# Second pass: factors turned by TensorE and multiplied from PSUM; node stage: P ahead of Q

## What is computed

```
z    = concat(h[src], h[dst], edge_feats) @ W.T + b          # 256 columns per edge
z    = (z - mean) * rsqrt(var + eps) * gamma + beta          # over all edges
msg  = sigmoid(z[:, :128]) * softplus(z[:, 128:])
x    = x + (h + zeros.at[src].add(msg))                      # summed by src
```

## Time and profile before

| | |
|---|---|
| median of 3 runs | 3818.71 us (3814.67 to 3823.7) |
| profiled execution | 3811.82 us, its span 3810.0 us |
| mean granted TensorE clock | 0.836 of 2.4 GHz |
| busy share | PE 68%, DVE 49%, ACT 37%, POOL 67% |
| chain that ended last, by engine | POOL 37%, PE 31%, issue 15%, DVE 7%, DMA 5%, ACT 3% |

### The profile page before, as it was taken

How to read it: one execution, slowest core, us unless ns; L and a number is a source line. 1 busy time by engine, 2 the same in 40 slices (tenths; PEclk the granted TensorE clock), 3 DMA queues, 4 the chain that set the end, 5 groups by cost and what they waited for, 6 DMA issues and landing times.

```text
span 3810.0 us, 64994 instructions
## 1 busy us (share of the span) xinstructions
PE 2572.3 (68%) x14952; PEld 1728.3 (45%) x14953; DVE 1875.5 (49%) x4083; ACT 1418.7 (37%) x2638; POOL 2552.8 (67%) x2545
## 2 busy tenths in 40 slices
PE   1788888778888885788888899972212113656348
PEld 1466666645555553344444444431111113555348
DVE  7555655555656566533333333343323234666448
ACT  3333333220000002322222222228877777777700
POOL 4477777467777660477777777755777777777730
PEclk9998999969989897999999999995555556887669
DMA  4233333335545451688888888877665555777358
GB/s 115 67 101 102 101 102 100 122 94 173 180 159 178 161 187 39 205 292 290 285 289 293 285 287 287 290 234 286 217 214 186 196 205 208 269 272 254 113 171 266
DMA packets 339096, 749.99 MB, mean 197 GB/s; under 512 B 66424, under 2 KB 130268, under 8 KB 333856
## 3 DMA queue, kind: packets, MB, share of 16 engines
q1 hardware_dynamic: 242656, 497.83, 37.8%
q0 software_dynamic: 93440, 218.82, 19.3%
q10 hardware_dynamic: 2880, 32.11, 2.2%
HBM read 465.29 MB, written 283.22 MB: 196 GB/s over the span
## 4 chain that ended last, share of the span: by engine, by line
POOL 37%; PE 31%; issue 15%; DVE 7%; DMA 5%; DVEq 3%; ACT 3%; POOLq 0%; SPq 0%; ACTq 0%
POOL m_tab L811 19%; POOL H L780 9%; PE PS L1554 9%; POOL arena L780 8%; PE PS L1564 8%; PE PS L1740 3%; PE PS L1627 2%; PE PS L1550 2%; DMA m_tab<-Q,pos_i 2%; DMA Q<-base_tab 1%; DVEq L1136 1%; PE PS L1609 1%; PE PS L1693 1%; PE PS L1719 1%; DVEq L409 1%
## 5 line engine op out<-in xcount | busy, mean ns | idle before, releaser
L780 POOL DMA_INDIRECT Q<-h_tab,src_i x960 | 954.8, 995 | 405.8 <-issue 273.7
L811 POOL DMA_INDIRECT m_tab<-Q,pos_i x784 | 833.7, 1063 | 275.2 <-issue 234.1
L1749 PE MATMUL PS<-ident,arena 128*128 128x128 f32 x784 | 196.2, 399 | 690.9 <-DVE arena L1452 608.4
L780 POOL DMA_INDIRECT arena<-p_tab,src_i x400 | 381.2, 953 | 262.8 <-DMA p_tab<-arena 141.2
L984 ACT ACTIVATE arena<-PS,LB 128x512 f32<-128x512 f32 x392 | 247.9, 683 | 746.7 <-PE PS L1724 746.7
L1564 PE MATMUL PS<-Q 128*128 x2684 | 420.0, 302 | 147.7 <-DVE Q L1138 65.0
L1749 PEld LDWEIGHTS PS<-ident,arena 128*128 128x128 f32 x784 | 129.0, 200 | 751.1 <-issue 529.0
L1564 PEld LDWEIGHTS PS<-Q 128*128 128x128 f32 x2684 | 355.3, 205 | 234.2 <-issue 229.9
L780 POOL DMA_INDIRECT H<-p_tab,src_i x384 | 363.9, 948 | 117.0 <-issue 116.1
L1724 PE MATMUL PS<-arena,WC 128*128 128x512 f32 x784 | 369.4, 594 | 0.0
L1719 PE MATMUL PS<-H,Q 128*128 x1464 | 352.7, 383 | 0.0
(11 more groups left out here) (231 smaller groups left out, 4351.8 us busy)
## 6 DMA issues: line engine op xcount, KB each, us to landing
z_tab<-arena SPq DMA_DIRECT2D x196, 512.0 KB
Q<-z_tab SPq DMA_DIRECT2D x196, 512.0 KB, 6.0
Q<-m_tab SPq DMA_DIRECT2D x234, 264.0 KB, 3.8
arena<-in_edge_t SPq DMA_DIRECT2D x196, 256.0 KB, 3.3
m_tab<-arena SPq DMA_DIRECT2D x48, 792.0 KB
m_tab<-src_i SPq DMA_DIRECT2D x112, 264.0 KB
arena<-dst_tab SPq DMA_DIRECT2D x196, 128.0 KB, 4.1
count_tab<-Q SPq DMA_DIRECT2D x11, 1568.0 KB
```

The source lines that it names most:

```text
L780: nc.gpsimd.indirect_dma_start(row(s, k), None, table, bass.IndirectOffsetOnAxis(src_i[:, t:t + 1], 0)).then_inc(landed[s], 16)
L811: nc.gpsimd.indirect_dma_start(m_tab, bass.IndirectOffsetOnAxis(pos_i[:, t:t + 1], 0), mrow[:, s, k, :], None).then_inc(ms.scattered[s], 16)
L1749: ins = turn(PS[:, 2 + q, t * P:(t + 1) * P], msg_t[:, q, t * P:(t + 1) * P], ident[:])
```

## The change

Node stage. TensorE makes all of P first (14 pieces of 4 and 3 tiles, 256 columns each) and then all of Q (21 pieces, 256 columns each, the blocks in the order 4, 5, 6, 0, 1, 2, 3), in three sets of two PSUM banks. The turned h stays whole in the arena (`ht_all`). VectorE adds h to X right after the layer norm, ahead of its part of Q, and the second rest of Q is written as part 2 in one instruction where there were two. GpSimd waits for the stored P and for `x_merged`; the first four groups are gathered into H, the next four into the arena, where each waits until the turned h under it is used up. The edge loads of pass 1 wait for nine pieces of Q.

Pass 2. ScalarE makes max(z, 0) itself (`positive`, a Relu into `core`). TensorE turns three things a group instead of one (`turn_parts`): the gate into banks 2 and 3, and into banks 0 and 1 the positive part and, added to it in PSUM by a plain multiplication with the identity, the logarithm. VectorE (`message`) copies the turned gate to SBUF, multiplies it with the sum in PSUM straight into `mrow`, and writes the source numbers. `scale_z`, `soften` and `take_rows` are gone. The seven output blocks have a buffer each.

```diff
             def turned_h(i):
                 act.wait_ge(pq.turned, i + 1)
-                if i >= 2:
-                    act.wait_ge(pq.product, len(SUBS) * (i - 1))
-                nc.scalar.copy(ht[:, i % 2, :], banks(0)).then_inc(pq.evicted, 1)
+                nc.scalar.copy(ht_all[:, i * NB:(i + 1) * NB, :]..., banks(0)).then_inc(pq.evicted, 1)
...
             gather_all(h_tab[1], conv_row, conv[1].group_done, CITER * CS, rows_landed[0:CS], DG)
             all_stored(pool, pq.p_stored)
+            pool.wait_ge(p1.x_merged, NI)
             gather_all(p_tab, p_row, p1.done, SL, rows_landed, 0)
...
+            def positive(d, s):
+                nc.scalar.activation(core[s], zin[:, s, GE:2 * GE], ACT.Relu, bias=bn[:, 11:12], scale=bn[:, 9:10]
+                                     ).then_inc(ms.relu_ready, 1)
...
-                    v.tensor_tensor(q_rest(c - 1), q_rest(c - 1), q_part(c - 1, 1), ALU.subtract
-                                    ).then_inc(dn.rest[1], 1)
-                    dve.wait_ge(dn.rest[1], SPLIT + c)
-                    v.tensor_copy(q_part(c - 1, 2), q_rest(c - 1)).then_inc(dn.part[2], 1)
+                    v.tensor_tensor(q_part(c - 1, 2), q_rest(c - 1), q_part(c - 1, 1), ALU.subtract
+                                    ).then_inc(dn.part[2], 1)
...
             def message(d, s):
                 g, q = group_of(d, s), s % 2
-                dve.wait_ge(ms.soft_ready, g + 1)
-                dve.wait_ge(ms.turned, g + 1)
-                v.tensor_tensor(msg_t[:, q, :], gate[:, s, :], soft[:, s, :], ALU.mult).then_inc(ms.msg_t_ready, 1)
+                dve.wait_ge(ms.turned, g + (RZ + 1))
+                if not (isinstance(d, int) and d == 0):
+                    dve.wait_ge(ms.scattered[s], eight_of(d) * (16 * GT))
+                v.tensor_copy(gate_rows[:, q, :], PS[:, 2 + q, :]).then_inc(ms.gate_taken, 1)
+                dve.wait_ge(ms.gate_taken, g + 1)
+                v.tensor_tensor(mrow[:, s, :, 0:F], PS[:, q, :].rearrange("p (a b) -> p a b", b=F),
+                                gate_rows[:, q, :].rearrange("p (a b) -> p a b", b=F), ALU.mult)
+                v.tensor_copy(mrow[:, s, :, F:F + 1].rearrange("p a b -> p (a b)"), columns(src_f, g)
+                              ).then_inc(ms.row_ready, 1)
...
-            def turn_msg(d, s):
+            def turn_parts(d, s):
                 g, q = group_of(d, s), s % 2
-                pe.wait_ge(ms.msg_t_ready, g + (RZ + 1))
+                pe.wait_ge(ms.relu_ready, g + (RZ + 1))
                 pe.wait_ge(ms.row_ready, g + 1)
                 for t in range(GT):
-                    ins = turn(PS[:, 2 + q, t * P:(t + 1) * P], msg_t[:, q, t * P:(t + 1) * P], ident[:])
+                    turn(PS[:, 2 + q, t * P:(t + 1) * P], gate[:, s, t * P:(t + 1) * P], ident[:])
+                for t in range(GT):
+                    mm(PS[:, q, t * P:(t + 1) * P], core[s][:, t * P:(t + 1) * P], ident[:], is_transpose=True,
+                       start=t == 0, stop=False, skip_group_check=True)
+                pe.wait_ge(ms.ln_ready, g + 1)
+                for t in range(GT):
+                    ins = mm(PS[:, q, t * P:(t + 1) * P], soft[:, s, t * P:(t + 1) * P], ident[:],
+                             start=False, stop=True, skip_group_check=True)
                 ins.then_inc(ms.turned, 1)
```

More of the change, by code:

```diff
@@ L772, in gather_all @@
                     s = (g - first) % depth
-                    if table is p_tab and g == SL:
-                        pool.wait_ge(p1.x_merged, NI)
+                    if table is p_tab and SL <= g < RP:
+                        last = (g - SL + 1) * GT * H2 // F - 1
+                        pool.wait_ge(pq.product, CP + len(SUBS) * (Q_ORDER.index(last // NB) + 1))
                     if g >= first + depth:
@@ L961, in _ @@
             turned_h(0)
-            for c in range(CH):
-                i, (j0, j1) = c // len(SUBS), SUBS[c % len(SUBS)]
+            for c in range(CP):
+                i, (j0, j1) = c // len(QUADS), QUADS[c % len(QUADS)]
+                if j0 == 0 and i + 1 < NI:
+                    turned_h(i + 1)
                 act.wait_ge(pq.product, c + 1)
@@ L966, in _ @@
                     act.wait_ge(pq.p_stored[i % 2], 16 * (i // 2))
-                nc.scalar.copy(p_s[:, i % 2, j0 * H2:j1 * H2].rearrange("p (j f) -> p j f", f=H2), pq_bank(c, 0)
+                nc.scalar.copy(p_s[:, i % 2, j0 * H2:j1 * H2].rearrange("p (j f) -> p j f", f=H2), p_bank(c)
                                ).then_inc(pq.p_ready, 1)
-                nc.scalar.copy(q_part(c, 0), pq_bank(c, 1)).then_inc(dn.part[0], 1)
-                if j0 == 0 and i + 1 < NI:
-                    turned_h(i + 1)
+            for c in range(CH):
+                act.wait_ge(pq.product, CP + c + 1)
+                nc.scalar.copy(q_part(c, 0), q_bank(c)).then_inc(dn.part[0], 1)
                 if c >= 1:
@@ L1014, in logarithm @@
                 nc.scalar.activation(soft[:, s, :], soft[:, s, :], ACT.Ln, bias=1.0).then_inc(ms.ln_ready, 1)
-            def take_rows(d, s):
-                g, q = group_of(d, s), s % 2
-                act.wait_ge(ms.turned, g + 3)
-                if not (isinstance(d, int) and d == 0):
-                    act.wait_ge(ms.scattered[s], eight_of(d) * (16 * GT))
-                nc.scalar.copy(mrow[:, s, :, 0:F], PS[:, 2 + q, :].rearrange("p (a b) -> p a b", b=F))
-                nc.scalar.copy(mrow[:, s, :, F:F + 1].rearrange("p a b -> p (a b)"), columns(src_f, g)
-                               ).then_inc(ms.row_ready, 1)
             def four(d, s, stage):
@@ L1487, in _ @@
                 dve.wait_ge(fin.turned, i + 1)
-                if i >= 3:
-                    dve.wait_ge(fin.out[i % 3], 16 * (i // 3))
-                v.tensor_tensor(outs[:, i % 3, :], banks(4 + i % 2 * 2), node_tiles(X, i), ALU.add
+                v.tensor_tensor(outs[:, i, :], banks(4 + i % 2 * 2), node_tiles(X, i), ALU.add
                                 ).then_inc(fin.added, 1)
@@ L1688, in _ @@
                 pe.wait_ge(pq.evicted, i + 1)
-                if c >= 2:
-                    pe.wait_ge(dn.rest[0], SPLIT + c - 1)
+                if c >= QB:
+                    pe.wait_ge(pq.p_ready, c - QB + 1)
                 for j in range(j0, j1):
-                    bank = PS[:, 2 + 3 * (c % 2) + j - j0, :]
-                    ins = mm(bank, ht[:, i % 2, j * F:(j + 1) * F], WAB[:], start=True, stop=True)
+                    ins = mm(p_bank(c)[:, j - j0, :], ht_all[:, i * NB + j, :], WAB[:, 0:H2], start=True, stop=True)
+                ins.then_inc(pq.product, 1)
+            pe.wait_ge(pq.p_ready, CP)
+            for c in range(CH):
+                t, n = pq_tiles(c)
+                if c >= QB:
+                    pe.wait_ge(dn.rest[0], SPLIT + c - QB + 1)
+                for j in range(n):
+                    ins = mm(q_bank(c)[:, j, :], ht_all[:, t + j, :], WAB[:, H2:2 * H2], start=True, stop=True)
                 ins.then_inc(pq.product, 1)
```

108 lines of the change are left out of this document (44 added, 64 removed).

## The result

| | before | changed |
|---|---|---|
| median of 8 runs each | 3815.36 us (3809.45 to 3823.7) | 3802.86 us (3792.84 to 3808.7) |
| ratio, 95% interval | | 0.9964 (0.9954 to 0.9974) |
| profiled execution's span | 3810.0 us | 3791.0 us |
| mean granted TensorE clock | 0.836 | 0.894 |

The change makes the kernel 12.5 us faster; 37 were forecast. So the profiles put 10.7 us on the change, and the medians 12.5.

The account below looks back on a forecast made before the run. GpSimd was taken to bound pass 1 (gathers) and pass 2 (scatters), with TensorE alone in the final sums. -26 - 35 + 26 - 2 = -37 gave 3775 us profiled, 3782 as median, range 3725 to 3822.

Parts of the forecast that it names:

- P ahead of Q, -26: Node stage: first gather of P 28.6 us earlier, net +3 from early gathers slowed and others freed, so 26 us saved.
- Q late: Rival, node stage: Q's pieces keep the old 2.5 us each, first slot freed 13 us late, 3795; chance 0.11.
- Pass 2 up to the sorted sums, -35: Scatters before the sorted sums: VectorE operations reading two SBUF tiles go, winning 35 of 36.9 us of scatter delay.
- The rival in which PSUM operations block as well: Rival, pass 2: VectorE's PSUM work blocks GpSimd as before, nothing gained from scatters, 3817; chance 0.09.
- The small four-column copy: VectorE, pass 2: would take the port lock shared with GpSimd, losing an estimated under 2 us of the 35.
- ScalarE's batch: Pass 2: sigmoid, size, Relu and table loads for four groups take 17.0 us against 20.3 for 16 scatters, so hidden.
- The sorted sums, +26: Sorted stretch: VectorE and TensorE wait on each other in a ring of 6.4 us a group; 486 us against 460.4.
- The clock rival: Sorted stretch: TensorE's clock stays 0.80, ring 7.45 us a group, 65 us more, 3847; chance 0.13.
- Ring hidden: Rival, sorted stretch: multiplications overlap better, GpSimd stays the bound, -23 in place of +26, 3733; chance 0.17.
- Output blocks, -2: Kernel's end: with seven buffers VectorE's waits for stored outputs go, the first 1.03 us, saving 2 us.
- a clock below 0.87: Sorted stretch: mean TensorE clock from which the change turns to a loss; stated as proof the prediction is wrong.

Follow-up runs that it names:

- two_sbuf: Changed kernel plus one VectorE product of 384 columns a group ahead of the sorted stretch, both inputs in SBUF; 3823.68 us, before 3819.65, one run each.
- psum_op: Changed kernel plus one VectorE product of 384 columns a group ahead of the sorted stretch, one input in PSUM; 3800.90 us, before 3819.65, one run each.
- fill8_e: Changed kernel plus eight unused 128-column multiplications on TensorE between a group's turning and its sums; short landings, 3777.01 us, 0.9907 of the kernel before.
- hot_first_e: Changed kernel with VectorE's one-hot matrices written ahead of its message; short landings 3736.18 us, 0.9790 of the kernel before; same kernel with long landings 1.0104 to 1.0118.

## Why the prediction was right or wrong

**P ahead of Q, -26: right.** -25.7 by the profiles. The gathers start 30.0 earlier (28.6 forecast) and lose 5.5 beside line 1347 (5.3 forecast; the line is VectorE's subtraction for part 2 of Q, with two SBUF inputs), while the loss beside `x_merged` is gone. Q's products end at 1547.3, and pass 1's first turning follows at 1553.47; the wait on Q's pieces was hidden, so the rival Q late did not come.

**Pass 2 up to the sorted sums, -35: right.** -36.7; the mean scatter is 437.92 / 452 = 0.969. two_sbuf and psum_op show the reason. The prediction named the wrong instruction beside its example, the scatter at 2606.27: line 1452 started 0.44 us behind that scatter, and the one ahead of it was line 1444, which also reads two SBUF tiles and is gone too, so the term didn't suffer:

```profile
2606.11 0.67 DVE L1444 SCALAR_TENSOR_TENSOR arena<-stats,arena 128x512 f32<-128x512 f32 x1
```

The rival in which PSUM operations block as well is dead. The small four-column copy cost nothing that the mean shows. ScalarE's batch stayed hidden, as forecast: TensorE waited 57.3 us for it in this stretch, GpSimd only 5.2 for rows.

**The sorted sums, +26: this is the step that failed.** It measured +51.4, and the 25.4 between are the missing gain. The mechanism was right link by link, and so was its size at full clock: 6.4 forecast for a round, 6.45 measured in fill8_e, and 486 forecast for the stretch, 486.3 measured there. That the stretch agrees to the microsecond is luck: the row of group 119 came 8.5 us into it and not 12, and the rounds from there to group 182 took 406.5 and not 403. What failed is "TensorE: a sum is ... 0.89", with the clock taken as full in every round. With the gap of 2.2 in each round, which the sum itself contained, the clock fell in 15 of 63 rounds, at 1.62 each: 24.3 us. Filling that gap gave 25.5 of it back.

**The clock rival was the right mechanism at two fifths of its size** (24.3 of its 65 us). It had 0.80 for the whole stretch, or full clock in the forecast, and nothing between. The measured mean is 0.94. Its rule for the price, TensorE's 4.2 us divided by the clock, would give 4.2 / 0.94 less 4.2, 0.27 a round, and 0.38 was measured (6.83 less 6.45): in the rows above the half clock lies on the sums and none of it on the gap, where it would cost nothing, and so it is with all fifteen (TensorE is busy 97 to 100 per cent of each fall). The case against it, that pass 1 keeps 0.99 with short gaps, compared gaps of another kind: 131 us of 989 there, a third of every round here. By the Trainium skill (TensorE: Matmul & The Clock Gate, the section on psum-queue depth-cycling) short idle spells between groups of matmuls make the clock swing; this case agrees, with 0.94 where the spell is 2.18 and 1.00 where it is filled to 0.39.

**Ring hidden: wrong for this order of instructions**, since TensorE waits for the one-hot and GpSimd for the rows. hot_first_e shows that nearly its gain (86 us forecast, 77.5 measured) is had by an order in which the one-hot matrices stand ahead of the message.

**Output blocks, -2: nothing.** VectorE's seven additions now run without a pause, but the end does not move: 14.3 us from the first of them to the end (3791.0 less 3776.68), 14.35 before (3810.0 less 3795.65). The wait went from a buffer to the landing of the last store: from the end of the last addition to the end of the kernel it is 6.7 us, where it was 4.1.

```profile
3776.68 7.60 DVE L1468 TENSOR_TENSOR Q<-PS,X 128x896 f32<-128x896 f32 x7 [1.08 <-PE PS L1769]
```

```profile
3795.65 3.26 DVE L1490 TENSOR_TENSOR Q<-PS,X 128x896 f32<-128x896 f32 x3 [1.08 <-PE PS L1777]
```

What I said would prove me wrong was a clock below 0.87 in the stretch. It was 0.94 in the steady part and 0.90 over the whole stretch, and the gain was still a third of the forecast: that threshold was set for a change of sign, too coarse to guard the size.

## What to carry to other kernels

When two engines are to hand work back and forth in each round, look at what stands behind the waiting instruction: here three one-hot matrices that needed nothing from the message stood behind it, and moving them ahead was worth 65 to 67 us with short landings, five times what the change itself gained. A ring that leaves TensorE idle for a third of each round is priced with the clock as part of the sum: work out the round at both clock levels and give the mixture its own chance. If the ring can't be opened, useless matmuls in the gap can pay (23 to 26 us here, with short landings). Here they filled 1.95 of a gap of 2.18; longer ones were not tried. And note the latency of landings beside every comparison: where a ring is bound by it, a change that gains with short ones can lose with long ones.

## What the runs showed of the hardware that was not expected

- TensorE idle for 2.18 us in rounds of 6.0 to 6.9: the clock fell to half for 3.4 us again and again, once in four groups mostly, each time while the engine was busy (97 to 100 per cent). With the gap down to 0.39 it didn't fall in any of the 63 rounds.
- A VectorE operation of 0.55 us with both inputs in SBUF cost GpSimd 0.10 us a time beside scatters (12.3 us over 118 operations), and the same operation with one input in PSUM nothing. Only operations that started ahead of a scatter, by up to 0.39 us, made it longer, by up to 0.39 us (two_sbuf).
- In six sets of runs of nine VectorE went on from a scatter's landing no sooner than some 31 us after the scatter's end (31.5 in hot_first) in place of 1.4, and the kernel before takes 15 to 17 per cent longer there. One chip number had both. A change can have the other sign: hot_first is 0.979 of the kernel before with short landings and 1.010 to 1.012 with long ones. In a ring of eight slots that are written again after landing, the latency is a term of the sum.
